# State steps of four state indices by 32 channels, and eight running averages on TensorE in blocks of 128 tokens

## What is computed

```python
# conditioning block, per sequence x[t, 256]
ctx   = causal_ema(x, tau_ctx)                        # h = alpha*h + x[t]
gate  = sigmoid(concat(x, ctx) @ Wg.T + bg)
gated = gate * x
mod   = sigmoid(gelu(x @ Wn1.T + bn1) @ Wn2.T + bn2)  # [t, 8]
temporal = sum over d in 0..7 of softmax_d(blend)[d] * causal_ema(gated * (0.5 + mod[:, d]), tau[d])
soma  = gelu(x @ Wsoma.T + bsoma)
y     = layernorm((soma * sigmoid(temporal @ Wtemp.T + btemp)) @ Wout.T)
# mixer, 512 inner channels, 16 state indices
xc, z = split(y @ W_in.T); xc = silu(causal_conv4(xc) + conv_b)
dt, B, C = split(xc @ W_x.T)                          # 64, 16, 16 columns
delta = softplus(dt @ W_dt.T + b_dt)
h[n]  = exp(delta * A[n]) * h[n] + delta * B[t, n] * xc[t]   # for n in 0..15
out   = ((sum over n of C[t, n] * h[n]) + D * xc) * silu(z) @ W_out.T
```

## Time and profile before

| what | value |
|---|---|
| median of three executions | 3804.92 us |
| the profiled execution: span from first to last instruction | 3793.6 us |
| busy share of the span: TensorE, VectorE, ScalarE, GpSimd | 91%, 60%, 41%, 17% |
| prologue, up to the first input of a state step | 129.7 us |
| from there to the end of the last state step | 1442 us |
| one sequence in the middle of them | 183.7 us |

### The profile page before, as it was taken

How to read it: one execution, slowest core, us unless ns; L and a number is a source line. 1 busy time by engine, 2 the same in 40 slices (tenths; PEclk the granted TensorE clock), 3 DMA queues, 4 the chain that set the end, 5 groups by cost and what they waited for, 6 DMA issues and landing times. The chain is left out here.

```text
span 3793.6 us, 37524 instructions
## 1 busy us (share of the span) xinstructions
PE 3438.3 (91%) x11356; PEld 1798.5 (47%) x11357; DVE 2286.6 (60%) x2808; ACT 1540.0 (41%) x2923; POOL 638.5 (17%) x768
## 2 busy tenths in 40 slices
PE   7798989889898986599979999999999999987996
PEld 4344443434343432266634444444444444445775
DVE  3699999999999999622214353535343444433334
ACT  3555546464646463133314242333333242323443
POOL 0000202020202021223300010110202020205772
PEclk9899999999999998799989999999999999998998
DMA  2122222222222223422130001010101010036557
GB/s 78 56 76 86 80 80 81 79 81 86 81 79 82 83 86 119 151 69 66 61 123 1 26 30 40 16 48 8 55 1 55 1 55 1 32 133 208 158 157 266
DMA packets 157913, 291.45 MB, mean 77 GB/s; under 512 B 27600, under 2 KB 84560, under 8 KB 156624
## 3 DMA queue, kind: packets, MB, share of 16 engines
q1 hardware_dynamic: 129216, 225.01, 18.4%
q0 software_dynamic: 20352, 57.17, 4.1%
q10 hardware_dynamic: 8208, 7.54, 0.6%
HBM read 195.74 MB, written 93.90 MB: 76 GB/s over the span
## 5 line engine op out<-in xcount | busy, mean ns | idle before, releaser
L1206 PE MATMUL ps<-hs,ident 128*128 128x512 f32 x1024 | 515.4, 651 | 123.7 <-DVE hs L1327 123.7
L1321 DVE TENSOR_TENSOR_SCAN hs<-dA,hs 128x2048 f32<-128x2048 f32 x128 | 565.5, 4418 | 7.0 <-DVE hs L1313 0.5
L427 POOL COPY rows<-slot 128x64 f32<-128x64 f32 x48 | 12.1, 282 | 2729.3 <-DVE new_pl L564 2704.2
L1886 PE MATMUL ps<-pT,V 128*128 128x512 f32 x1024 | 450.7, 593 | 0.9 <-DVE pT L2054 0.9
L1271 ACT ACTIVATE dA<-dl,w_An 128x511 f32<-128x511 f32 x512 | 325.9, 709 | 261.0 <-DVE hs L1321 260.5
L1206 PEld LDWEIGHTS ps<-hs,ident 128*128 128x128 f32 x1024 | 209.9, 209 | 412.9 <-issue 257.8
L1313 DVE TENSOR_TENSOR hs<-u,bb 128x2048 f32<-128x2048 f32 x128 | 292.4, 2285 | 20.0 <-PE ps L1206 19.9
L1886 PEld LDWEIGHTS ps<-pT,V 128*128 128x128 f32 x1024 | 189.6, 190 | 221.1 <-issue 214.7
L1327 DVE TENSOR_TENSOR hs<-hs,cb 128x2048 f32<-128x2048 f32 x128 | 290.0, 2266 | 0.0
L1456 POOL DMA_INDIRECT slots<-og,idt x232 | 241.8, 1042 | 260.3 <-DVE og L1544 199.9
L423 POOL DMA_INDIRECT sorted<-rows,new_pl x192 | 274.8, 1431 | 63.6 <-issue 44.8
(11 more groups left out here) (353 smaller groups left out, 5394.6 us busy)
## 6 DMA issues: line engine op xcount, KB each, us to landing
bb<-bcd SPq DMA_DIRECT2D x128, 256.0 KB, 3.5
cb<-bcd SPq DMA_DIRECT2D x128, 256.0 KB, 3.2
xg<-sorted SPq DMA_DIRECT2D x232, 136.0 KB, 2.1
slots<-zeros SPq DMA_DIRECT2D x136, 128.0 KB, 3.2
qrg<-slots SPq DMA_DIRECT2D x32, 512.0 KB, 17.6
W0u<-modd SPq DMA_DIRECT2D x40, 256.0 KB, 3.4
rg<-slots SPq DMA_DIRECT2D x32, 256.0 KB, 4.7
w_Lr<-in_Lora SPq DMA_DIRECT2D x8, 576.0 KB, 3.9
```

What stands on the lines that cost most here:

```text
L1206: ins = pe.matmul(ps[:, j, :], ident[:, :], m.hs[:, N % 3, j, :], start=False, stop=(N % NS == NS - 1))
L1321: dve.tensor_tensor_scan(state, m.dA[:, N % 2].rearrange("p j t -> p (j t)"), state, 0.0, ALU.mult, ALU.add).then_inc(s_h, 1)
L1886: ins = pe.matmul(ps[:, 6 + j, :], V[:, m, h * D + j * P:h * D + (j + 1) * P], pT[:, i % 2, h % 2, m, :], start=(h == 0 and m == 0), stop= ...
```

## The change

**State steps.** Partitions now hold four state indices by 32 channels, and the four chunks of a tile are four groups of 32 channels. A step N covers four of the 16 state indices for one quarter (128) of the channels; a group G of four steps finishes that quarter. There are 128 steps as before, of the same tile size. The sum over n is made on TensorE with a matrix S4 of 128 x 32 that adds the four state indices: four products of 32 columns, each into 32 other partitions of one PSUM bank. The quarters take banks 0, 1, 2 in turn. `gate` becomes four single pieces at n = 5, 9, 13 and 0 of the next sequence.

**delta and u** must be laid out four times over 32-channel lines. They are stored to DRAM (`dld`, `ud`) and read back for each group: 4 + 4 DMAs of 256 KB, four groups for each sequence.

**Averages.** All eight go by the turned path, in blocks of 128 tokens: a product of each block with a 128 x 128 matrix of decays, a product of the block with the last column of that matrix (`block_ends`, 32 output columns, of which one for each d is not zero), and one product `carry_ends` that adds what earlier blocks carry in. The VectorE averages, the DRAM trip of `mod` and the strips go.

**Order.** The pieces of b+1 move: averages n = 0 to 7, temporal gate 8, out product and variance 9, `y` at 9, input product 10, convolution 10 to 12, ranks 12 (dt, B and C in one product of 96 columns), delta 13 (VectorE makes delta and u at 13), z 15. The hidden product, the modulation, the context and the gates are made for b+2 at n = 8 to 15. On TensorE the pieces of a step now stand ahead of add_state, and `variance_product` behind it.

The core of the diff:

```diff
-                        for j in range(JI):
-                            ins = pe.matmul(ps[:, j, :], ident[:, :], m.hs[:, N % 3, j, :], start=False,
-                                            stop=(N % NS == NS - 1))
+                        for q in range(GROUP):
+                            ins = pe.matmul(ps[LINE * q:LINE * (q + 1), N // GROUP % 3, :], S4[:, :], m.hs[:, N % 3, q, :],
+                                            start=False, stop=(N % GROUP == GROUP - 1))
                         ins.then_inc(s_acc, 1)
...
+        def turn_gated(pe, c, k, d, h):
+            if d == 0 and h == 0:
+                pe.wait_ge(c_gd, k + 1)
+            elif k or d or h:
+                pe.wait_ge(c_tge, 4 * NTR * k + 4 * d + 2 * h)
+            for q in (2 * h, 2 * h + 1):
+                for j in range(DC):
+                    ins = pe.matmul(ps[:, 3, q % 2 * D + j * P:q % 2 * D + (j + 1) * P],
+                                    c.gated[:, j, q * P:(q + 1) * P], mix[:, j, d, :], start=True, stop=True)
+            ins.then_inc(c_tgp, 1)
+
+        def average(pe, c, k, d, j):
+            pe.wait_ge(c_tge, 4 * NTR * k + 4 * (d + 1))
+            for q in range(TT):
+                pe.matmul(ps[:, 6 + j, q * P:(q + 1) * P], c.turned[d % 2][:, q, j * P:(j + 1) * P], c.decay[:, d, :],
+                          start=(d == 0 and q == 0), stop=False)
+
+        def block_ends(pe, c, k, d):
+            if d == 0:
+                pe.wait_ge(c_sm, DC * (k + 1))
+            for q in range(TT - 1):
+                ins = pe.matmul(ps[LINE * q:LINE * (q + 1), 5, 0:D], c.last[:, d, :], c.turned[d % 2][:, q, :],
+                                start=(d == 0), stop=(d == NTR - 1))
+            ins.then_inc(c_part, 1)
+
+        def carry_ends(pe, c, k):
+            pe.wait_ge(c_ends, k + 1)
+            for j in range(DC):
+                pe.matmul(ps[:, 6 + j, P:T], c.ends[:, j * P:(j + 1) * P], Rm[0:3 * LINE, :],
+                          start=False, stop=True).then_inc(c_avg, 1)
...
+        def rank_product(pe, m, k):
+            pe.wait_ge(m_xs, JI * (k + 1))
+            product(pe, ps[0:DTR + 2 * NS, 4, :], [(Wxm[:, i, :], m.xs[:, i, :]) for i in range(JI)], m_dt)
...
+        def scale_turned(act, c, k, d, h):
...
+            act.wait_ge(c_tgp, 2 * NTR * k + 2 * d + h + 1)
+            for q in (2 * h, 2 * h + 1):
+                act.activation(c.turned[d % 2][:, q, :], ps[:, 3, q % 2 * D:(q % 2 + 1) * D], ACT.Copy,
+                               scale=modT[:, q, d:d + 1]).then_inc(c_tge, 1)
...
-            dst, done = (m.bb, s_bl) if which == 0 else (m.cb, s_cl)
-            sp.dma_start(dst[:, n % 2, :], bcd[b % 2, NS * which + n].partition_broadcast(P)).then_inc(done[n % 2], 16)
+            row = NS * which + GROUP * (N % GROUP)
+            sp.dma_start(dst[:, N % 2, :], bcd[N // NS % 2, row:row + GROUP, :].unsqueeze(1).to_broadcast([GROUP, LINE, T])
+                         ).then_inc(done[N % 2], 16)
...
+        def store_groups(sp, c, k):
...
+            sp.wait_ge(m_dlr, k + 1)
+            sp.dma_start(dld[0], c.dl[:, 0, :]).then_inc(m_st0, 16)
+            sp.wait_ge(m_u, k + 1)
+            sp.dma_start(ud[0], c.u[:, 0, :]).then_inc(m_st0, 16)
+            sp.dma_start(dld[1:JI].rearrange("j p t -> p j t"), c.dl[:, 1:JI, :]).then_inc(m_st, 16)
+            sp.dma_start(ud[1:JI].rearrange("j p t -> p j t"), c.u[:, 1:JI, :]).then_inc(m_st, 16)
+
+        def spread_group(sp, m, G):
+            j = G % JI
+            sp.wait_ge(m_st if j else m_st0, 32 * (G // JI + 1))
+            if G >= 2:
+                sp.wait_ge(s_da, GROUP * GROUP * (G - 1))
+            for n in range(GROUP):
+                sp.dma_start(m.dl[LINE * n:LINE * (n + 1), G % 2], dld[j].rearrange("(q c) t -> c q t", c=LINE)
+                             ).then_inc(s_dl[G % 2], 16)
+            if G >= 2:
+                sp.wait_ge(s_bm, GROUP * (G - 1))
+            for n in range(GROUP):
+                sp.dma_start(m.u[LINE * n:LINE * (n + 1), G % 2], ud[j].rearrange("(q c) t -> c q t", c=LINE)
+                             ).then_inc(s_ul[G % 2], 16)
...
+                        elif n == 8:
+                            if kc is not None:
+                                temporal_product(pe, c, kc)
+                            if ke is not None:
+                                hidden_product(pe, c, ke)
+                        elif n == 9 and kc is not None:
+                            cond_out_product(pe, c, kc)
...
                         for n in range(NS):
-                            if NS * b + n:
+                            tasks(b, n)
+                            if n:
                                 add_state(NS * b + n - 1)
...
+                            if n == 9 and kc is not None:
+                                variance_product(pe, c, kc)
...
+                        elif n == 9:
+                            decays_ahead()
+                            if kc is not None:
+                                cond_scale(act, c, kc)
...
+                        elif n == 9:
+                            if b >= 0:
+                                gate(b, 1)
+                            if kc is not None:
+                                cond_ready(dve, c, kc)
...
+                        elif n == 13:
+                            if kc is not None:
+                                delta_ready(dve, m, c, kc)
+                            if b >= 0:
+                                gate(b, 2)
```

More of the change, by code:

```diff
@@ L732, in cond_tensors @@
[L732 to L739 removed]
+            c.cx, c.wg = room[:, 0:2, :], room[:, 2:4, :]
@@ new lines, in gate_ready, with soma_ready @@
+        def gate_ready(act, c, k, j):
+            if j == 0 and k >= 3:
+                act.wait_ge(r_pl, (2 + M0.K) * (k - 2))
+            act.wait_ge(c_gate, DC * k + j + 1)
+            act.activation(c.wg[:, j, :], ps[:, 3 if j == 0 else k % 3, :], ACT.Sigmoid, bias=bg[:, j:j + 1]).then_inc(c_wg, 1)
+        def soma_ready(act, c, k):
+            for j in range(DC):
+                act.wait_ge(c_soma, DC * k + j + 1)
+                act.activation(c.soma[:, j, :], ps[:, 4 + j, :], ACT.Gelu, bias=bsoma[:, j:j + 1]).then_inc(c_sm, 1)
@@ new lines, in cond_scale @@
+        def cond_scale(act, c, k):
+            for j in range(DC):
+                act.wait_ge(c_out, DC * k + j + 1)
+                act.activation(c.oc[:, j, :], ps[:, 6 + j, :], ACT.Copy).then_inc(c_oc, 1)
+                act.activation(c.sq[:, j, :], ps[:, 6 + j, :], ACT.Square).then_inc(c_sq, 1)
+            act.wait_ge(c_var, k + 1)
+            act.activation(c.lnv, ps[:, 6, :], ACT.Ln, bias=epst[:, :]).then_inc(c_lnv, 1)
+            act.wait_ge(c_lnv, k + 1)
+            act.activation(c.rstd, c.lnv, ACT.Exp, scale=-0.5).then_inc(c_std, 1)
@@ new lines, in copy_turned, with mixer_counts, route_exps @@
+        def copy_turned(act, v, k, h):
+            if h == 0 and k:
+                act.wait_ge(M0.listed, 16 * TT * M0.K * k)
+            act.wait_ge(r_tr, TT * DC * k + 4 * (h + 1))
+            act.activation(v.rows[:, 0, 2 * h:2 * h + 2, 0:D], halves(4), ACT.Copy).then_inc(r_rd if h else r_ra, 1)
+        def mixer_counts(pe, v, k):
+            pe.wait_ge(r_rd, k + 1)
+            count_choices(pe, M0, v, 4, k)
+        def route_exps(act, v, k):
+            act.wait_ge(r_ex, 2 * k + 1)
+            act.activation(v.pb[:, :, :], v.pb[:, :, :], ACT.Exp, scale=1.0 / TEMP).then_inc(r_ex, 1)
@@ L1103, in mixers @@
             v, c = m.v, m.c
-            c.strips += (m.xs[:, 0, :],)
-            c.turned += (y[:, :, :].rearrange("p a (s c) -> p (a s) c", c=D),)
-            f.strips = c.strips
+            f.decay, f.last_row, f.spare = c.decay, c.last, c.spare
             last = NS * B
@@ L1354, in _ @@
                     for b in range(B):
-                        k, kc = behind(b), next_up(b)
                         for n in range(NS):
```

964 lines of the change are left out of this document (571 added, 393 removed).

## The result

The changed kernel takes 3853.55 us (median of 4; 3852.04 to 3859.19) against 3804.56 us (4) for the kernel before: ratio 1.0135, 95% interval 1.0122 to 1.0147. It is slower by 49.0 us. The forecast was 3764 us and the range ended at 3850.

The account below looks back on a forecast made before the run. VectorE was taken to pace the state steps, TensorE following closely. Span 3793.6 - 64 (state steps) + 29 (prologue) - 6 (end) = 3752.6 us; median 11.3 above, 3764 us; own range 3730 to 3795, full range 3695 to 3850.

Parts of the forecast that it names:

- state steps: 128 scan steps over eight sequences: six sequences gain 9.6 us each and sequence 0 about 6, together 64 us less.
- prologue: Work before the first state step, without cover: averages +18, one rank product less -3, DRAM trip +13.5 to 14.5; sum +29 us.
- end: After the last state step: shorter sums and one gate piece left of four cut the gate's 8.0 us wait; -6 us.
- The trip of delta and u through DRAM: Stores, then spread loads, at 387 GB/s: about 13.5 us behind u, hidden in steady order with 2.6 us to spare.
- Rival C: Sums overlap, but new waits are longer (late DRAM trip or cold TensorE): period 178 to 183, 3790 to 3835 us; chance 0.12.
- 16 x 1.4: Averages before the first state step: 16 halves turned and scaled one after the other, 1.4 us of exposed time each.
- Column products: TensorE's four 32-column products into four quarters of PSUM overlap: 1.1 us a sum, against 3.4 in turn.
- A: Rival: the four column products on TensorE run in turn, 3.6 us a sum; about 3955 us; chance 0.17.
- B: Rival: only neighbouring products overlap or weight loads stand bare, 2.0 to 2.3 us a sum; 3813 us; chance 0.10.
- Own work of VectorE: VectorE's busy time per sequence falls from 180.3 to 162.5 us as the averages' multiplications and scans leave it.
- Wait for the scale: At n = 9 VectorE waits for the variance chain on ScalarE and TensorE before y: 6.2 us a sequence.
- Wait for delta: From y to delta, a 43 us chain against 37.6 us of VectorE work: wait at n = 13 of 5.4 us a sequence.

Follow-up runs that it names:

- interleaved partitions: Changed kernel with state index n, channel c on partition 4c + n instead of 32n + c, so loads of delta and u reach 128 partitions: 3747.90 us.

## Why the prediction was wrong

The forecast of the span was 3752.6 us; 3852.6 came. The 100.0 us between them: state steps 83.2 (predicted -64, came +19.2), prologue 11.2 (predicted +29, came +40.2), end -1.1 (predicted -6, came -7.1), later stages 6.7 (predicted 0). The last is scatter, as far as the runs show: from the last `xm` to the end it is 2210.4 us before and 2217.1 after, but 2211.3 without the loads and 2217.3 with interleaved partitions. So is the allowance of 11.3 us between span and median, 1.0 here: the profiled execution of before was a fast one. It hides 10 us of the miss, which is 89.6 us against the median.

**The step that failed** is the rate in "The trip of delta and u through DRAM". I took 387 GB/s from the earlier trace rows for "1.5 MB of stores 4 us, 2 MB of loads 5.4 us". The row shows the peak of a mix, and no row of before shows a load onto 32 partitions; it was an operation without a row, and I gave its rate one value. Only the trip of the prologue had bounds (9 and 20 us, and its 17.5 lie inside); the steady order had none. At 210 GB/s the loads of a sequence (4 groups of 2 MB) need 40 us of all engines, not 22. The second half of the failure is who pays. I weighed the trip against its own reader, `into(16)`, and found 2.6 us to spare; at 17.4 us it outran that cover in seven sequences, but by 9.7 us in all. Of the rows of B and C I wrote that they are "queued behind the waits of SP", followed only cb(15), which has 27 us to spare, and put the rest at nothing. The rows of B, needed in every step, go through the same engines, and the sum has no term for what they wait while 2 to 4 MB stand ahead of them: 82.5 us. Rival C named "the trip lands 5 us late each time"; the lateness was of that kind, but spread over 27 waits on another tile, and its top, 3835, too low. With the loads left out or fast the whole comes to 3755 or 3748, inside the forecast's own range, so that one cause carries the miss. That 3764 is near is in part luck. With interleaved partitions the span is 3752.9 us, the forecast 3752.6, but prologue +37.9 for +29, later stages +6.9 for 0, state steps -78.0 for -64 and end -7.5 for -6 cancel.

**The prologue.** Its trip took 17.5 us behind u (152.4 to 169.9) and not 13.5; with fast loads it is 12.8. The rest is in the averages, predicted +18, came +25.2 (`y` at 105.87, before at 80.70). "16 x 1.4" for turn and scaling was too small at the start: TensorE's timeline,

```profile
26.57 2.05 PE L805 MATMUL ps<-w_mix,W0u 128*128 128x128 f32 x8 [4.96 <-DVE ones_b L303]
29.60 2.08 PE L805 MATMUL ps<-w_mix,W0u 128*128 128x128 f32 x8 [0.99 <-ACT W0u L903]
32.61 2.08 PE L805 MATMUL ps<-w_mix,W0u 128*128 128x128 f32 x8 [0.93 <-ACT W0u L903]
35.62 2.08 PE L805 MATMUL ps<-w_mix,W0u 128*128 128x128 f32 x8 [0.93 <-ACT W0u L903]
...
46.59 1.16 PE L805 MATMUL ps<-w_mix,W0u 128*128 128x128 f32 x8 [0.95 <-ACT W0u L903]
```

has four turns at 2.05 to 2.08 us, 3.0 us a round with the scaling, where the same turn takes 1.16 later. TensorE had idled 5 us before the first; a duration of nearly twice the later one is the lower of the clock's two levels (1.2 for 2.4 GHz), and the granted clock from 30 to 50 us is 0.75, from 70 to 100 us 1.00. Four rounds at 3.0 and not 1.4 would make 6.4 of the 7.2 us; that is an estimate from these rows, and no run tests it.

**What held.** Column products: taken at 1.1 us, 1.06 where TensorE is at speed, 1.33 in the mean; block ends 0.6, measured 0.63. A and B fell with it, and the strict reading of the Trainium skill's rule on loads ("TensorE: Matmul & The Clock Gate", Part 3), under which a sum would take 2.0 us; all these products use all rows, and they overlap. Own work of VectorE: 162.5, measured 162.5. Wait for the scale: 6.2, measured 6.1. Wait for delta: 5.4, measured 5.7. End: -6, measured -7.1; the gate that waited 8.0 us waits 2.1. The gain that these steps promise for the state steps, 64 us, is there once the loads are fast: phase 1422.9 to 1344.9, 78 us. The six middle sequences give 65.4 of it (57.6 in the sum), sequence 0 gives 11.6 (6 in the sum), and the last 1.0. One reading of the rows was too wide: not every product of before uses all rows, the one for delta (`W0u,w_Wdt 64*128`) has 64; those of the 4.48 us do.

## What to carry to other kernels

Price a transfer by its form, not by its bytes: how many partitions it writes and how many entries its outermost dimension has, and take the rate from a row of the same form; if none exists, give it a wide lower bound: the forms in this case ran at 390, 210 and 100 GB/s. Then ask of every other transfer in the same queue who reads it next and how much stands ahead of it, above all of the small ones that each step needs. And a step moved "out of the way" on an engine is free only if it was filling nothing: look at what the engine would idle for in its old place.

## What had not been expected of the hardware

- A load onto 32 partitions runs at about 210 GB/s with a DMA share of 9 tenths or more; the same bytes onto 128 at 380 to 415 with the same share. The share tells that engines are occupied, not that they move what they can.
- A DMA whose outermost dimension is four keeps the share at 2 tenths and the rate at 98 to 102 GB/s; used for the loads it cost 270 us more than the slow form.
- Issuing slows when queues are full: a DMA that is issued in 0.53 us takes 2.23 to 3.67 us behind the loads.
- Four float32 products of 32 columns take 1.33 us a set in the mean (1.06 at speed), four full ones 4.03 (515.4 us for 128 sets): a threefold gain, worth 171 us in this kernel with loads onto 128 partitions and 97 with loads onto 32.
